# Attention scores on float32 high and low parts, two heads in 64-row tiles, with masks as 64-row products and maxima over two banks

## The reference, cut to what matters

```python
# x [2, 1024, 128] float32; 16 heads of 8 columns; 8 experts, two for each token
h = layernorm(x) * (1 + ca) + sa
Q = (h @ W_dq) @ W_uq ; K = (h @ W_dkv) @ W_uk ; V = (h @ W_dkv) @ W_uv   # 16 heads x 8
scores = einsum('bqhd,bkhd->bhqk', Q, K) / sqrt(8), causal
x = x + ga * (softmax(scores) @ V) @ W_o
h = layernorm(x) * (1 + cb) + sb
x = x + gb * (shared expert + the two best of 8 experts, weighted)
```

## Time and profile before

| | |
|---|---|
| Time, median of 3 executions | 430.55 us (429.49 to 431.08) |
| Span of the profiled execution, the only time recorded for it | 455.7 us |
| Busy in it: PE, DVE, ACT, POOL | 422.1, 319.5, 268.1, 150.0 us |
| Products of maxima (L1685), of scores (L1716), of weighing (L1740), busy | 116.0, 112.6, 77.9 us |
| Masked maxima (L1282), plain maxima (L1286), busy | 111.5, 82.9 us |
| Exponentials (L941), busy | 156.2 us |

### The profile page before, as it was taken

The page is one execution under the profiler, slowest core; times in us unless marked ns, Lnnn a source line. Parts: engine busy times, 40 slices in busy tenths (PEclk is TensorE's granted clock), DMA queues, the critical chain, the costliest instruction groups (busy, mean ns, idle before and its releaser), DMA issues.

```text
span 455.7 us, 9455 instructions
## 1 busy us (share of the span) xinstructions
PE 422.1 (93%) x2963; PEld 242.9 (53%) x2963; DVE 319.5 (70%) x1185; ACT 268.1 (59%) x611; POOL 150.0 (33%) x244
## 2 busy tenths in 40 slices
PE   6989899999999999999999999999959779999984
PEld 3434423353443544454544434337747569999944
DVE  5768855788887987889797886355866435555646
ACT  3557344556666767675666576967446254555661
POOL 2246200026010020106556434231664743333520
PEclk9998855999999999999999999999989959999999
DMA  5245160034040210400400000960112223210126
GB/s 146 65 141 124 34 192 3 1 101 146 1 106 2 58 51 0 106 3 0 108 7 19 21 21 23 315 149 13 43 46 54 76 65 83 60 40 26 36 85 216
DMA packets 28796, 31.78 MB, mean 70 GB/s; under 512 B 4827, under 2 KB 23363, under 8 KB 28243
## 3 DMA queue, kind: packets, MB, share of 16 engines
q1 hardware_dynamic: 25959, 25.82, 20.0%
q0 software_dynamic: 2272, 4.67, 3.0%
q10 hardware_dynamic: 516, 0.69, 0.5%
HBM read 21.04 MB, written 9.85 MB: 68 GB/s over the span
## 4 chain that ended last, share of the span: by engine, by line
PE 71%; DVE 13%; issue 4%; DMA 4%; ACT 2%; another core or an unknown queue 2%; POOL 1%; SPq 1%; ACTq 0%; DVEq 0%; POOLq 0%
PE oacc L1740 15%; PE mx L1685 12%; PE sc L1716 12%; PE sc L1873 7%; PE oacc L1888 7%; DVE mxp L1286 4%; DVE masked L1282 3%; PE sc L1721 2%; PE mx L1840 2%; PE mx L1829 2%; PE mx L1749 1%; PE mx L1864 1%; PE sc L1829 1%; DMA S<-first_q_parts 1%
## 5 line engine op out<-in xcount | busy, mean ns | idle before, releaser
L941 ACT ACTIVATE pr<-sc 128x512 f32<-128x512 f32 (+1 forms) x295 | 156.2, 580 | 93.0 <-PE sc L1716 45.3
L1282 DVE CUSTOM_DVE_ANT_0 masked<-mx,later 128x128 f32<-128x128 f32 (+3 forms) x256 | 111.5, 485 | 19.4 <-PE mx L1685 18.7
L1685 PE MATMUL mx<-S 72*128 72x512 bf16 (+3 forms) x384 | 116.0, 344 | 6.4 <-DVE mxp L1282 2.2
L1716 PE MATMUL sc<-S 75*128 75x512 bf16 (+3 forms) x371 | 112.6, 339 | 0.7 <-ACT pr L941 0.6
L1286 DVE TENSOR_REDUCE mxp<-mx 128x1 f32<-128x512 f32 x128 | 82.9, 685 | 23.5 <-PE mx L1685 23.1
L1740 PE MATMUL oacc<-pr,vb 128*32 128x512 f32 (+3 forms) x768 | 77.9, 515 | 0.0
L1011 ACT ACTIVATE pr<-sc,bcur 128x128 f32<-128x128 f32 x156 | 44.5, 369 | 33.4 <-PE sc L1873 18.4
L1716 PEld LDWEIGHTS sc<-S 75*128 75x128 bf16 x371 | 35.3, 100 | 51.2 <-issue 28.6
L1685 PEld LDWEIGHTS mx<-S 72*128 72x128 bf16 x384 | 35.0, 101 | 48.0 <-DVE mxp L1282 19.2
L783 POOL DMA_INDIRECT token_results<-S,xrow x39 | 38.5, 988 | 61.7 <-DVE S L1432 59.6
L1888 PE MATMUL oacc<-vb,pr 128*128 128x128 f32 x312 | 42.8, 283 | 5.2 <-ACT pr L1011 5.2
(11 more groups left out here) (294 smaller groups left out, 499.1 us busy)
## 6 DMA issues: line engine op xcount, KB each, us to landing
S<-k_parts SPq DMA_DIRECT2D x21, 192.0 KB
S<-q_parts SPq DMA_DIRECT2D x42, 96.0 KB
xrow<-slot_rows SPq DMA_DIRECT2D x39, 64.5 KB, 1.9
S<-in_we SPq DMA_DIRECT2D x1, 2048.0 KB, 9.7
S<-in_we SPq DMA_DIRECT2D x4, 512.0 KB, 10.4
parts<-token_results SPq DMA_DIRECT2D x4, 512.0 KB, 5.2
x_sb<-in_x SPq DMA_DIRECT2D x4, 256.0 KB, 3.9
out_y<-attn SPq DMA_DIRECT2D x4, 256.0 KB, 2.3
```

Of the source, the lines that this page charges most:

```text
L941: act.activation(pr[:, group % NBUF, h:h + n, at:at + w], src, ACT.Exp, scale=float(DK) ** -0.5).then_inc(s["exp_done"], 1)
L1282: ins = dve.tensor_tensor_reduce(masked[:, d % 2, w * m:w * m + w], unit[a][:, w * m:w * m + w], later[:, HALF - w:HALF], 1.0, LOWEST, ALU ...
L1685: ins = pe.matmul(dst[:, w * m:w * m + w], S3[0:CROSS, r3, 1, q:q + P], S3[0:CROSS, r3, 0, kk:kk + w], start=(m == 0), stop=True, skip_gro ...
L1716: ins = pe.matmul(dst[:, w * m:w * m + w], S3[0:CROSS + 3, r3, 0, kk:kk + P], S3[0:CROSS + 3, r3, 1, q:q + w], start=(m == 0), stop=True, ...
```

## The change

Q and K are split into two float32 parts instead of three of bfloat16, the high one rounded to the format `float32r` by ACT, the low one the remainder, formed by DVE (the first four projections) or POOL. The products read them as `float32r`. A head then needs 32 rows (2 x 2 parts x 8), one row of zeros, and two rows for the maximum in two parts: 33 rows for a maximum, 35 for a score. Two of a task's four heads lie in partitions 0 to 63 (`side` 0) and two in 64 to 127 (`side` 1), so that a product takes a tile of 64 rows of the array. A max unit is now one or two heads of *both* sides, in two banks of four (`mx` has 4, `sc` 3, `oacc` 1), and DVE reduces both banks at once. There are 20 max units in a task (before 38, reduced by 48 operations and 32 reads of the accumulator) and 40 score units (before 38). Masks on maxima and on scores are products of 64 rows (`rows_of`, `stairs`), two for each diagonal block and head. Weighing is by single groups everywhere, and has one bank. The transposed maximum is copied out by ACT instead of DVE. A slot is loaded by eight DMAs.

```diff
-QW = HQ * HALF
+QW = PAIR * HALF
-            n = HALF // w if w < 384 else 1
+            n = 2 if w <= 256 else 1
-            out += [(c, j, h, n, q0, w, P * j == q0) for h in range(0, HQ, n)]
+            out += [(c, j, side, h, n, q0, w, P * j == q0) for h in range(0, PAIR, n) for side in range(2)]
-AHEAD = 20
-MAXES_AFTER = [2] * 4 + [3] * 4 + [2] * 2 + [1] * 5 + [2 if g % 4 == 0 else 1 for g in range(28)]
+AHEAD = 12
+EXTRA_MAXES = 8
+FILLERS = 3
+SPLIT = 2
...
-            single = group < NG or group >= NG * (tasks - 1)
-            pair = 1 if single else 2
+            pair = 1
...
-        S3 = sb("S3", [P, 3, 2, HQ * S], BF16)
+        with nc.sbuf_tensor("operands", [P, 3, 2, 2 * QW], F32) as S3:
+            S3r = S3[:, :, :, :].bitcast(F32R)
-        oacc = ctx.enter_context(nc.psum_tensor("oacc", [P, 2, 512], F32))
+        mx = ctx.enter_context(nc.psum_tensor("mx", [P, 4, 512], F32))
+        oacc = ctx.enter_context(nc.psum_tensor("oacc", [P, 1, 512], F32))
...
             def load_k(t, cols, sem):
-                src = kd[b, u, :, :, :, cols].rearrange("d a h n -> (d a) h n")
-                for a in range(3):
-                    sp.dma_start(S3[24 * a:24 * a + 24, r3, 0, :].rearrange("r (h n) -> r h n", h=HQ)[:, :, cols],
-                                 src).then_inc(sem, 16)
+                for side in range(2):
+                    src = kd[b, u, :, :, PAIR * side:PAIR * side + PAIR, cols].rearrange("d a h n -> (d a) h n")
+                    for a in range(2):
+                        at = SIDE * side + 2 * DK * a
+                        sp.dma_start(S3[at:at + 2 * DK, r3, 0, :].rearrange("r (h n) -> r h n", h=PAIR)[:, :, cols],
+                                     src).then_inc(sem, 16)
...
             def max_unit(t, k, a):      # DVE
-                if diagonal:
-                    for m in range(n):
-                        ins = dve.tensor_tensor_reduce(
-                            masked[:, d % 2, w * m:w * m + w], unit[a][:, w * m:w * m + w], later[:, HALF - w:HALF],
-                            1.0, LOWEST, ALU.add, ALU.max, mxp[:, c, place, h + m, i - 4 * c:i - 4 * c + 1])
+                own = mx[:, HELD["max", t, k][0]:HELD["max", t, k][0] + 2, 0:n * w]
+                dve.tensor_reduce(sides(mxp[:, c, place, :, i - 4 * c])[:, :, h:h + n],
+                                  own.rearrange("p s (m w) -> p s m w", m=n), AX_X, ALU.max).then_inc(s["aux_free"], 1)
...
             def max_scores(t, k, a):    # PE
+                    for side in (1, 0):
+                        dst = bank[HELD["max", t, k][side]]
+                        ins = pe.matmul(dst[:, w * m:w * m + w], operand(r3, side, ONES_AT, 1, q, P),
+                                        operand(r3, side, ONES_AT, 0, kk, w), start=(m == 0), stop=True,
+                                        skip_group_check=(m > 0))
+                if diagonal:
+                    for part in range(2):
+                        for side in (1, 0):
+                            ins = pe.matmul(dst[:, :, at:at + SIDE], rows_of[own, 0, part, :], stairs[own, 0:1, :].broadcast_to([SIDE, n, SIDE]),
+                                            start=False, stop=True, skip_group_check=True)
...
             def weigh(t, k):            # PE
-                if j == 0 and t >= 1:
-                    pe.wait_ge(s["o_done"], 2 * t + c - 1)
+                if j == 0 and 2 * t + c:
+                    pe.wait_ge(s["o_done"], 2 * t + c)
```

More of the change, by code:

```diff
@@ L230, in adaln_layer @@
     BY_DVE = [x for x in AUX if x not in ON_ACT]
-    LENT, BACK, task = {}, {}, None
-    for kind, t, k in ORDER:
-        if kind == "out" and k == 0:
-            task = t
-        elif (kind, t, k) in SPARE_BANK:
-            LENT[kind, t, k] = task
-            BACK[task + 1] = (kind, t, k)
+    LAST_HELD = [x for x, banks in HELD.items() if MX[3] in banks][-1]
     FREED = {x: n + 1 for units in (BY_ACT, BY_DVE) for n, x in enumerate(units)}
-    DIAGONAL = [(t, k) for t in range(T) for k in range(NM) if MAXU[k][6]]
-    RING = 3
-    NLOAD = 9
+    NLOAD = 8
     TOK = B * S
@@ L283, in adaln_layer @@
         identb = sb("identb", [P, P], BF16)
-        after = sb("after", [P, HQ, P], BF16)
-        later = sb("later", [P, HALF], F32)
-        masked = sb("masked", [P, 2, HALF], F32)
+        warmb = sb("warmb", [P, HALF], BF16)
+        stairs = sb("stairs", [P, 2, SIDE], BF16)
+        rows_of = sb("rows_of", [P, 2, 2, P], BF16)
         iota8 = sb("iota8", [P, NE], F32)
@@ L482, in store_parts @@
                 u0 = 0 if b else 1
-                for part in range(3):
+                for part in range(2):
                     sp.wait_ge(*part_done(part, QK.index((b, 0, 1))))
@@ L1623, in _ @@
             warm(2)
-            pe.matmul(mx[:, 0, 0:2 * P], identb[:, :], after[:, 0:2, :].rearrange("p h n -> p (h n)"), start=True, stop=True)
+            pe.matmul(bank[0][:, 0:2 * P], identb[:, :], warmb[:, 0:2 * P], start=True, stop=True)
             pe.wait_ge(s["wqkv_ready"], 1)
@@ new lines, in max_scores @@
+                    kk = S * (h + m) + k0
+                    for side in (1, 0):
[4 more added lines that the diff above has]
+                if diagonal:
+                    for part in range(2):
+                        for side in (1, 0):
+                            dst = bank[HELD["max", t, k][side]][:, 0:n * w].rearrange("p (m w) -> p m w", m=n)
+                            at = w - P + SIDE * part
+                            own = slice(SIDE * side, SIDE * side + SIDE)
+                            ins = pe.matmul(dst[:, :, at:at + SIDE], rows_of[own, 0, part, :], stairs[own, 0:1, :].broadcast_to([SIDE, n, SIDE]),
+                                            start=False, stop=True, skip_group_check=True)
@@ L1718, in score_unit @@
                                     skip_group_check=(m > 0))
                 if diagonal:
-                    ins = pe.matmul(dst[:, 0:n * w].rearrange("p (h n) -> p h n", h=n)[:, :, 0:P], identb[:, :],
-                                    after[:, 0:n, :], start=False, stop=True, skip_group_check=True)
+                    own = slice(SIDE * side, SIDE * side + SIDE)
+                    for part in range(2):
+                        ins = pe.matmul(dst[:, 0:n * w].rearrange("p (m w) -> p m w", m=n)[:, :, SIDE * part:SIDE * part + SIDE],
+                                        rows_of[own, 1, part, :], stairs[own, 1:2, :].broadcast_to([SIDE, n, SIDE]), start=False, stop=True,
+                                        skip_group_check=True)
@@ L1902, in _ @@
                     max_scores(t, k, a)
-                    fill(sc[:, 2, :], FILLERS.get((t, k), 0))
+                    if t == 0 and k < AHEAD - 1:
+                        fill(FILLERS)
                 elif kind == "turn":
```

442 lines of the change are left out of this document (203 added, 239 removed).

## The result

The changed kernel takes 614.24 us (median of four executions, 600.11 to 626.47) against 430.81 us for the kernel before (four, 429.49 to 433.30). The ratio is 1.394, with an interval of 1.385 to 1.403. Two of the four executions, 626 us, show a lower mean granted clock than the other two (0.63 against 0.66), and the ratio leaves them out. The profiled execution took 600.11 us, with a span of 598.4 us. The prediction said 398.0 us, 374 to 428, and faster with a chance of 0.83. It was wrong by half of the time before, on the other side.

What follows compares the result with a forecast made beforehand. PE was taken to bound a task (29.0 of 29.5 us); after the change PE 22.1, DVE 22.0 and ACT 20.9 us make 25.5 us a task, so 430.55 - 33 = 398 us, range 374 to 428 us.

Steps and rivals of the forecast that it cites:

- 8 x 22.7 us of maxima become 8 x 20.5 us ... At 86% this is 220 us: DVE's busy time from 24 to 283 us falls from 210 to 189 us, 220 us at 86% busy.
- Rival 1: PE waits in many small pieces and the clock falls more often; two stretches of 11.4 us each, 421 us; chance 12%.
- the granted clock is 0.50 over whole tasks: One of three signs in the profile by which the prediction would be wrong.
- Together: A task with PE 22.1, DVE 22.0, ACT 20.9 us takes 25.5 us at 86% busy, bounds 23.8 and 29.
- Maxima and scores: PE's products in a task, two tiles abreast: 72 times 512 columns by 0.11 us, 7.9 us instead of 15.8.
- no engine has room: Engines in a task wait for each other through two pairs of banks for maxima and three for scores; 86% taken.
- Masks: 96 small products of a task on PE: 2.2 us, bounds 1.4 and 5.4, before 1.8 us.
- Weighing: 12 single groups instead of six pairs on PE in a task: 10.65 us, 1.5 us more.
- DVE: DVE's work in a task: 22.0 us instead of 24.67, a reduction of two banks 1.13 us.
- Rival 5: DVE alone bounds a task: 23.8 us a task, 386 us; counted inside the forecast, without a chance of its own.
- Rival 4: Next group waits for ACT's copy, or the transposed maximum comes late: 28.5 us a task, 420 us; chance 9%.
- The start: Before the first maxima and while waiting for Q of the second half: 1 us given back at either place.

Runs made afterwards that it cites:

- e2_rows64: The changed kernel with all 64 rows of a tile in each product of maxima and scores, added rows zero: 469.04 us, ratio 1.084 to the kernel before.
- the streams: The layer left out for eight dense streams of products of different rows and formats, from high and low clock; 88 float32r products of 35 rows take 10.27 us.
- LAG = 4: The changed kernel with 64 rows and warm(42), weighing after the fourth score unit instead of the third: 454.42 us, ratio 1.053 to the kernel before.
- OUT = 4: The LAG = 4 kernel with the transposes of a finished half one score unit later: 453.87 us.
- e11_two_banks: The LAG = 4 kernel with two banks of scores instead of three, the third idle until the experts: 490.99 us, ratio 1.134 to the kernel before.
- e5_rows64_warm: The changed kernel with 64 rows in products of maxima and scores and 42 instead of 18 fillers before the first maxima: 459.0 us, ratio 1.067.
- LAG = 3: The changed kernel with 64 rows and warm(42), weighing still after the third score unit: 459.0 us, ratio 1.067 to the kernel before.

## Why the prediction was wrong

**The step that failed first is the clock.** "8 x 22.7 us of maxima become 8 x 20.5 us ... At 86% this is 220 us" takes the granted clock as 1.00 but for half a stretch of 27 us. Rival 1 named the mechanism (PE waits in pieces, the clock falls) and gave it 12% and two stretches, 23 us. In truth the waits only start it. I took from the earlier trace rows that a stretch ends after 27 us; in the changed kernel the low level lasts some 270 us (27 to 300 us) and then another 130 (334 to 464), 400 us where the forecast had half a stretch, and its products had gone from 72, 75 and 128 rows (masks and fillers) to 33, 35 and 64. The run e2_rows64 changed nothing but the rows of products (with what zeroes and loads them), and the clock came back. Weighing is over 128 rows in both kernels, and in the streams it brought the clock back alone; among products of few rows it wasn't enough. The prediction had these numbers before it and read rows only as speed. It did name the sign of its own failure, "the granted clock is 0.50 over whole tasks".

**The second step that failed is "Together".** PE 22.1, DVE 22.0, ACT 20.9 us were to make 25.5 us. At the full clock a task takes 31.20 us, with `LAG = 4` 30.14 us, and with `OUT = 4` besides 29.13 us. By term:

- *Maxima and scores*, 0.11 us for each 512 columns: right in a dense stream (0.227 us a pair), wrong in its place. In the round of 512 columns the sum gives 0.88 us for eight products and 1.10 for the weighing, 1.98 us; the round takes 2.67. The last score product before a weighing costs 0.43 us instead of 0.11; the other seven take 1.24 us (138.14 to 139.38) instead of 0.77, the wait for a bank among them.
- *The banks.* The sum had three banks of scores as "no engine has room" and a flat 86%. e11_two_banks and the row with 0.61 us show that ACT runs dry beside each weighing. At 86% the round would be 2.30 us; 0.37 us more in five rounds are 1.9 of the 4.6 us that a task (30.14 us) is over the forecast. The wait for ACT's copy is about 1.0 us more. The rest, some 1.7 us, I haven't separated.
- *Masks*: 2.2 us predicted, 1.7 measured. *Weighing*: 1.00 us to the next start, as in the earlier trace rows.
- *DVE*: three reductions in a row took 3.63 us, 1.21 each, for 1.13 predicted (its share of a round, 2.36 of 2.67 us, leaves 0.3 us); DVE bounds nowhere. Rival 5 did not come up.
- *Rival 4* (waits eat it, 28.5 us a task) was the nearest to what is left at the full clock. The larger part comes through the banks of scores, which it didn't name. Of its two places, ACT's copy of a finished half does cost 1.0 us a task, but it is the transposes that wait for it and not the next group.

**The start.** It was to give back 1 us. The first maxima came at 26.30 us instead of 24.13, behind 3.26 us of waiting for K. In time this cost 2 us, but the clock also fell behind it.

The Trainium skill (TensorE: Matmul & The Clock Gate, Why this matters for your kernels) advises against PE-idle gaps between bursts. The wait of 3.26 us and the fall behind it agree. The 270 us that follow at 0.50 have hardly a wait in them, so here the advice covers the fall and not what it cost.

As to the sign: with the clock brought back the kernels are still 23 to 28 us slower than before. By the estimate made for e5_rows64_warm, at the full clock it would be about 20 us with `LAG = 3`, 14 or 15 with `LAG = 4` and 9 to 11 with `OUT = 4` besides. The later start is a large part of what is left: maxima begin at 30.7 to 30.8 us in these runs. Of that 4.4 us belong to the rows of zeros and not to the change, whose own maxima began at 26.30. The task itself is no longer a loss with `OUT = 4` (29.13 against 29.53 us), but neither is it the 25.5 us that was forecast. Whether the change would pay at the full clock without the zeroing at the start was not tried. The time that the change frees on DVE is not what was short.

## What to carry to other kernels

Before a product is cut down to few rows, ask what else PE runs beside it: if most of its products use few rows, one wait can put the clock down for most of the stage (270 us here), and the page shows an engine that is 100% busy at half speed. Rows of zeros cost no time on PE (88 products of 35 rows took 10.27 us, of 64 rows 10.28) and can buy the clock back, though filling them delays the start. Look at PEclk before looking at busy time, and when two orders of work are compared, look at a task at the full clock and at the granted clock of each execution, since a gain in one can hide behind a loss in the other (`OUT = 4`). And a sum of busy times by engine says little where two engines hand three banks to and fro: add up one round from starts, with who holds which bank, and count a product that stands alone before a change of tiling by what it takes there (0.43 us, not 0.11).

## What the runs showed of the hardware

- Dense `float32r` products over 35 rows on one side of the array lost the full clock after some 5 us without any gap; on both sides they kept it for 10 us, but did not regain it from the low level in 19 us (`float32r`) and 24 us (bfloat16). 72 rows of bfloat16 in one tile did not regain it in 23 us; 64 rows on both sides did in about 6 us (`float32r`) and 3 us (bfloat16).
- The added rows needed no data: in e2_rows64 rows 35 to 63 of a tile are zero on both sides, and the clock still came back from 0.50 to 1.00.
- `float32r` products of 512 columns on two 64-row tiles took 0.233 us a pair (44 pairs in 10.27 us), and one over 128 rows also 0.233 us (56 in 13.07 us); four float32 column tiles took 12.22 us for 14 rounds, 0.87 us a round, near the 0.85 us that the prediction took as the work of a group.
